# A recurrent stage with the squares of its Newton chain on ScalarE, mixes of 1024 columns, and TensorE's products and transposes of a slot in blocks

## The reference

```python
def step(h, _):
    h = h + 0.01 * jnp.tanh(h)
    h = h * jax.nn.sigmoid(h)
    h = _layernorm(h, ln_w, ln_b)
    h = jnp.einsum('bsc,dc->bsd', h, W) + b
    return (h, None)
x, _ = jax.lax.scan(step, x, None, length=N_ITERS)
...
x = x + _L1_ffn_ref(_layernorm(x, axis=-1), L1_ffn_ln_w, L1_ffn_ln_b, L1_ffn_W, L1_ffn_b)
```

## Time and profile before

| | us |
|---|---|
| median of 3 runs | 3229.25 (3229.11 to 3229.91) |
| the profiled execution, its own time | 3229.77 |
| its span | 3228.0 |
| first three layers, and the start of the recurrent one | 0 to 1806 |
| recurrent layer, step 0 | 1806 to 1894 |
| steps 1 to 29 | 1894 to 3175 |
| last pass | 3175 to 3228 |

### The profile page before, as it was taken

How to read it: one execution, slowest core, us unless ns; L and a number is a source line. 1 busy time by engine, 2 the same in 40 slices (tenths; PEclk the granted TensorE clock), 3 DMA queues, 4 the chain that set the end, 5 groups by cost and what they waited for, 6 DMA issues and landing times. The chain is left out here.

```text
span 3228.0 us, 67245 instructions
## 1 busy us (share of the span) xinstructions
PE 3034.4 (94%) x16801; PEld 2092.0 (65%) x16801; DVE 2831.7 (88%) x8856; ACT 2382.6 (74%) x4988; POOL 1722.1 (53%) x1101
## 2 busy tenths in 40 slices
PE   6999896999999899999999489999999999999997
PEld 4666665888888577777777355555555555555556
DVE  4777776888888788888888779999999999999997
ACT  4666664444444577777777699999999999999993
POOL 2444444333332121211211058899898888888886
PEclk9999997999999999999999589999999999999999
DMA  4000000000000000000000035555555555555557
GB/s 130 17 19 16 16 16 14 1 0 0 0 0 0 25 14 10 13 12 11 13 10 4 3 132 195 198 184 188 198 190 184 197 195 184 190 199 188 187 197 245
DMA packets 135071, 290.03 MB, mean 90 GB/s; under 512 B 12081, under 2 KB 69601, under 8 KB 135009
## 3 DMA queue, kind: packets, MB, share of 16 engines
q1 hardware_dynamic: 118112, 280.89, 25.7%
q10 hardware_dynamic: 16896, 8.39, 0.9%
HBM read 278.88 MB, written 10.35 MB: 90 GB/s over the span
## 5 line engine op out<-in xcount | busy, mean ns | idle before, releaser
L1077 POOL TENSOR_TENSOR d_g<-d_g,d_rb 128x1024 f32<-128x1024 f32 x480 | 1121.1, 2371 | 269.6 <-DMA d_rb<-d_rstd_rows 269.6
L1265 PE MATMUL d_p_y<-d_g,d_w_main 128*128 128x512 f32 x1856 | 960.9, 599 | 0.0
L1279 PEld LDWEIGHTS d_p_gt<-ident,d_g 128*128 128x128 f32 x3840 | 466.0, 142 | 527.7 <-ACT d_g L1324 365.1
L1142 DVE BATCH_NORM_STATS2 d_stats<-d_p_gt 128x6 f32<-128x256 f32 x1920 | 712.7, 407 | 24.1 <-PE d_p_gt L1279 24.1
L1324 ACT ACTIVATE d_g<-d_th,d_bias 128x512 f32<-128x512 f32 x928 | 670.2, 722 | 67.1 <-DVE d_th L1135 37.3
L1135 DVE SCALAR_TENSOR_TENSOR d_th<-d_th,d_p_y 128x512 f32<-128x512 f32 x960 | 638.0, 665 | 4.4 <-ACT d_th L1320 4.3
L1320 ACT ACTIVATE d_th<-d_p_y,d_bias 128x512 f32<-128x512 f32 x928 | 621.7, 670 | 1.3 <-PE d_p_y L1265 1.2
L1279 PE MATMUL d_p_gt<-ident,d_g 128*128 128x128 f32 x3840 | 592.0, 277 | 0.0
L514 ACT ACTIVATE a_prob<-a_masked,a_neg_max 128x128 f32<-128x128 f32 x1024 | 327.4, 391 | 111.5 <-DVE a_neg_max L334 111.4
L434 PE MATMUL a_p_s<-a_k_heads,a_q_t 128*128 128x512 f32 x768 | 397.4, 599 | 0.5 <-DVE a_k_heads L310 0.5
L451 PEld LDWEIGHTS a_p_pv<-a_v_ones,a_prob_t 128*128 128x128 f32 x3072 | 373.7, 192 | 10.7 <-issue 10.3
(11 more groups left out here) (170 smaller groups left out, 4399.5 us busy)
## 6 DMA issues: line engine op xcount, KB each, us to landing
d_rb<-d_rstd_rows SPq DMA_DIRECT2D x480, 512.0 KB, 5.5
a_adj_in<-in_adj_dram SPq DMA_DIRECT2D x64, 256.0 KB, 2.8
out_dram<-d_out_sb ACTq DMA_DIRECT2D x32, 256.0 KB, 3.3
d_rstd_rows<-d_rstd_row SPq DMA_DIRECT2D x120, 16.0 KB, 1.4
m_w_sb<-in_L_ffn_w_dram SPq DMA_DIRECT2D x2, 512.0 KB
x_sb<-in_x_dram SPq DMA_DIRECT2D x1, 256.0 KB, 2.9
a_w_raw<-in_L_gnn_Wq_dram SPq DMA_DIRECT2D x2, 64.0 KB, 2.1
a_w_raw<-in_L_gnn_Wk_dram SPq DMA_DIRECT2D x2, 64.0 KB, 2.1
```

The lines of the kernel that those rows point to most:

```text
L1077: nc.gpsimd.tensor_tensor(g[:, c, :], g[:, c, :], rb[:, buf, :], ALU.mult).then_inc(s_gs, 1)
L1142: ins = nc.vector.bn_stats(stats[:, q % 2, (j * CT + t) // 2].rearrange("p a s -> p (a s)"), p_gt[:, t * P:(t + 2) * P].rearrange("p (a c) ...
L1265: nc.tensor.matmul(p_y[:, c % 2, cols(u)], w_main[:], g[:, c, cols(u)], start=True, stop=True).then_inc(s_y, 1)
L1279: ins = nc.tensor.transpose(p_gt[:, t * P:(t + 1) * P], g[:, c, t * P:(t + 1) * P], ident[:])
```

## The change

VectorE's chain for the reciprocal square root has nine steps instead of ten, by other constants, and steps 2, 4 and 6 of them are squares on ScalarE (`newton_square`), one after the silus of a slot. VectorE mixes a slot in one instruction of 1024 columns, after both tanhs. ScalarE runs tanh u0, tanh u1 of slot s, then silu u0, silu u1 of slot s-1. TensorE runs both products of a slot, then the transposes u0 of slot s-2, in one slot of four the transpose of the reciprocal square roots, then the transposes u1. GpSimd begins scaling when all of x is normalised. The last step's reciprocal square roots are not spread: `last_product` takes the unscaled state, and `add_x` multiplies while it adds, in four instructions of 128x128 per unit instead of one of 128x512; `out_sb` has eight buffers.

```diff
-    CHAIN, XCHAIN, PLACES = 10, 12, 3
+    SPREADS = ALL_GROUPS - GROUPS
+    CHAIN, XCHAIN, PREP = 9, 12, 11
+    PLACES = {(0, 2): 0, (1, 0): 1, (1, 2): 3, (2, 2): 5, (3, 2): 7, (4, 0): 8}
+    ACT_PLACES = {(1, 0): 2, (2, 0): 4, (3, 0): 6}
-    OUTS = 4
+    OUTS = 8
...
-            with eng.Fori(2, ITERS) as i:
+            with eng.Fori(2, ITERS - 1) as i:
                 body(i)
+            body(ITERS - 1)
             body(ITERS)
...
             @block.gpsimd
+                pool.wait_ge(s_xn, CHUNKS * UNITS)
+                pool.wait_ge(s_prep, PREP)
                 with pool.Fori(1, CHUNKS + 1) as i:
                     for c in range(CHUNKS):
                         scale(i, c)
-                    pool.wait_ge(s_prep, 10)
-                    pool.wait_ge(s_xn, CHUNKS * UNITS)
...
-                def mix(s, b, u):
-                    dve.wait_ge(s_th, units(s, u))
+                def mix(s, b):
+                    dve.wait_ge(s_th, units(s, UNITS - 1))
+                    nc.vector.scalar_tensor_tensor(out=th[:, b], in0=th[:, b], scalar=0.01, in1=p_y[:, b],
+                                                   op0=ALU.mult, op1=ALU.add).then_inc(s_u, 1)
...
                 def add_x(o, u):
+                    for t in range(UT):
+                        tile = u * UT + t
+                        ins = nc.vector.scalar_tensor_tensor(
+                            out=out_sb[:, n % OUTS, t * P:(t + 1) * P], in0=p_y[:, o % 2, tile * P:(tile + 1) * P],
+                            scalar=rstd[:, q, o % GC * CT + tile:o % GC * CT + tile + 1], in1=x_sb[:, o * CT + tile, :],
+                            op0=ALU.mult, op1=ALU.add)
...
-                        if live(s - 1):
-                            mix(s - 1, (c - 1) % 2, 1)
-                        elif last(i):
-                            add_x(c - 1, 1)
-                        newton_part(i, c, 0)
                         if live(s - 2):
                             statistics(s - 2, (c - 2) % CHUNKS, 0)
-                        newton_part(i, c, 1)
+                        newton_part(i, c, 0)
                         if live(s):
-                            mix(s, c % 2, 0)
+                            mix(s, c % 2)
                         else:
                             add_x(c, 0)
+                            add_x(c, 1)
+                        newton_part(i, c, 1)
                         if live(s - 2):
                             statistics(s - 2, (c - 2) % CHUNKS, 1)
                         newton_part(i, c, 2)
...
                 def last_product(s, c, u):
-                    pe.wait_ge(s_gs, s - CHUNKS + 1)
+                    pe.wait_ge(s_g, units(s - CHUNKS, u))
...
-                            if live(s - 2):
-                                transpose_g(s - 2, (c - 2) % CHUNKS, u)
-                        k = GROUPS * i + (c - 9) // GC
-                        if c % GC == 1 and live_group(k):
-                            transpose_rstd(k)
+                        if live(s - 2):
+                            transpose_g(s - 2, (c - 2) % CHUNKS, 0)
+                        k, q = GROUPS * i + (c - 10) // GC, (c - 10) // GC % GROUPS
+                        if c % GC == 2 and spread_group(k):
+                            transpose_rstd(k, q)
+                        if live(s - 2):
+                            transpose_g(s - 2, (c - 2) % CHUNKS, 1)
...
+                def newton_square(k, q, n):
+                    act.wait_ge(s_nw, CHAIN * k + n)
+                    if n == 4:
+                        ins = nc.scalar.activation(off, vy2, ACT.Square, bias=centre[:])
+                    else:
+                        ins = nc.scalar.activation(y2[:], rstd[:, q, :], ACT.Square, scale=1.0 if n == 2 else CUBIC)
...
-                        if live(s):
-                            tanh(s, c % 2, 0, col)
-                        if live(s - 1):
-                            silu(s - 1, (c - 1) % CHUNKS, 1, 0.0 if isinstance(i, int) and s - 1 < CHUNKS else bias[:])
+                        for u in range(UNITS):
+                            if live(s):
+                                tanh(s, c % 2, u, col)
+                        for u in range(UNITS):
+                            if live(s - 1):
+                                silu(s - 1, (c - 1) % CHUNKS, u, 0.0 if isinstance(i, int) and s - 1 < CHUNKS else bias[:])
+                        newton_part(i, c, 0)
...
-                        if live(s):
-                            tanh(s, c % 2, 1, col)
-                            silu(s, c, 0, col)
```

More of the change, by code:

```diff
@@ L974, in recurrent_ffn @@
         stats = sb("stats", [P, 2, GTILES // 2, 2, 3])
[L975 to L976 removed]
+        rstd = sb("rstd", [P, GROUPS, GTILES])
+        y2 = sb("y2", [P, GTILES])
+        centre = sb("centre", [P, 1])
         rstd_row = sb("rstd_row", [GTILES, 2, P])
@@ L988, in recurrent_ffn @@
         p_rt = p_row[0:GTILES, 0:P]
-        v, work, v_x, work_x = (p_nw[:, n * GTILES:(n + 1) * GTILES] for n in range(4))
+        v, vy2, off, v_x, work_x = (p_nw[:, n * GTILES:(n + 1) * GTILES] for n in range(5))
         s_load = sem("weights_loaded")
@@ L1027, in live_group, with spread_group @@
             return not isinstance(k, int) or 0 <= k < ALL_GROUPS
+        def spread_group(k):
+            return not isinstance(k, int) or 0 <= k < SPREADS
         def iterations(eng, body):
@@ L1087, in _ @@
                                             ALU.add).then_inc(s_xb, 1)
-                with pool.Fori(CHUNKS + 1, ITERS + 1) as i:
+                with pool.Fori(CHUNKS + 1, ITERS) as i:
                     for c in range(CHUNKS):
@@ L1211, in body @@
                             if c in (0, 1, 4, 5, 8, 9):
-                                for n in range(c % GC * 6, c % GC * 6 + 6):
+                                for n in range(c % GC * 6, min(c % GC * 6 + 6, XCHAIN)):
                                     newton_of_x(1 + c // GC, n)
@@ L1220, in _ @@
                     stats_of_x(GC + c)
-                    for n in range(3 * c, 3 * c + 3):
+                    for n in range(3 * c, min(3 * c + 3, XCHAIN)):
                         newton_of_x(0, n)
@@ L1236, in _ @@
                 link(nc.vector.tensor_copy(bias_bc[:], p_gt[:, P:2 * P]))
+                link(nc.vector.memset(centre[:], -5.0 / 3.0))
                 iterations(dve, body)
-                dve.wait_ge(s_xb, CHUNKS)
-                add_x(CHUNKS - 1, 1)
             @block.tensor
@@ L1254, in bank_taken @@
                     else:
-                        wait(pe, s_u, units(s - 2, u))
+                        wait(pe, s_u, s - 1)
                 def transpose_x(c, u):
@@ L1322, in silu, with newton_part @@
                 def silu(s, c, u, col):
-                    act.wait_ge(s_u, units(s, u))
+                    act.wait_ge(s_u, s + 1)
                     nc.scalar.activation(g[:, c, cols(u)], th[:, c % 2, cols(u)], ACT.Silu, bias=col).then_inc(s_g, 1)
+                def newton_square(k, q, n):
[4 more added lines that the diff above has]
+                        ins = nc.scalar.activation(y2[:], rstd[:, q, :], ACT.Square, scale=1.0 if n == 2 else CUBIC)
+                    ins.then_inc(s_nw, 1)
+                def newton_part(i, c, place):
+                    k, q = GROUPS * i + (c - 5) // GC, (c - 5) // GC % GROUPS
+                    n = ACT_PLACES.get(((c - 5) % GC, place))
+                    if n is not None and live_group(k):
+                        newton_square(k, q, n)
                 def store(o, u):
```

61 lines of the change are left out of this document (26 added, 35 removed).

## The result

The changed kernel takes **3242.98 us** (median of 6 runs, 3241.78 to 3245.20) against 3229.18 (6 runs, 3226.34 to 3231.66): ratio 1.0044, 95% interval 1.0032 to 1.0057. It is slower by 14 us, where the prediction had 3222.0 and a range up to 3238. The profiled execution took 3243.27, its span is 3241.4.

A forecast was written before the change was run, and what follows sets the result against it. VectorE, never waiting in steps 1 to 29, bounds the kernel at 11.07 us per group; after the change a loop gives 11.02. Sum -5.8 + 6 + 1 - 8.5 = -7.3 from 3229.25: 3222.0 us, range 3207 to 3238.

The forecast's parts named there:

- The loop: Steps 1 to 29: TensorE and VectorE wait on each other through one-slot p_gt; 5.42 us per two slots, 10.84 per group.
- 0.05 until the weight load begins: Handover from the end of VectorE's statistics u1 to TensorE's weight load, 0.05 us, read from 12.43 to 12.48.
- The small transpose: TensorE's transpose of the reciprocal square roots, between the two blocks; sticks out a little, within a shared +0.03 per group.
- the chain's first step: VectorE's first reciprocal-square-root step waits for statistics just issued; sticks out, within a shared +0.03 per group (0 to 0.2).
- the branch: Turn of TensorE's instruction loop, once in 16 slots: 0.2 sticks out, +0.05 us per group, between 0 and 0.08.
- ScalarE's load: Steps 1 to 29: three squares add 0.67 to 10.22, giving 10.89 us per group, between 10.64 and 11.38.
- rival 2: The loop does not bind, a wait being released earlier; ScalarE's 10.89 per group decides, 3207 us; chance 0.08.
- The ends: Step 0 +6 us from ScalarE's order and +1 from GpSimd's later scaling; last pass 44.5 instead of 53, -8.5.
- Rival 1: Mix, branch and small transpose cost 0.02 to 0.11 per group more: 3224 to 3235 us, no visible change; chance 0.34.
- rival 3: ScalarE becomes the bound: at 0.385 per square a group costs 11.38, giving 3264 us; chance 0.07.
- Rival 4: TensorE's queue pays more, register work behind waits delaying the product: group 11.2, 3243 us; chance 0.09.
- The rule of the Trainium skill: VectorE's wide mix takes 1.19 us; if the next instruction waited for all, +0.16 per group, near 3240.

The follow-up runs named there:

- stats_first: Changed kernel with VectorE's statistics u1 of slot s-2 ahead of the wide mix of slot s instead of behind it: 3159.01 us, ratio 0.9782 to the kernel before.
- wait_order: Changed kernel with the two waits of transpose_g swapped, first for the statistics, then for the silu: 3243.40 us, ratio 1.0043 to the kernel before.
- interleaved: Changed kernel with TensorE running product u0, transposes u0 of s-2, product u1, then transposes u1: 3298.55 us, ratio 1.0215 to the kernel before.

## Why the prediction was wrong

**The loop** was read rightly: its place, its members and that it binds before any load. What failed is its length. Per turn, predicted and measured in the rows above:

| | predicted | measured |
|---|---|---|
| statistics u1 until done | 0.74 | 0.755 |
| until the weight load | 0.05 | 0.115 |
| load to product | 0.49 | 0.495 |
| products, transposes, start | 2.36 | 2.355 |
| statistics u0, wide mix | 1.78 | 1.80 |
| two slots | 5.42 | 5.52 |

The step that failed is "0.05 until the weight load begins": two thirds of the error of 0.10 come from there, and with them the sign of the result. The term was read from one handover, and that one has another form than the loop's. The trace of the kernel before has two forms (2000 to 3000). 678 weight loads of transposes have the wait for the statistics on an instruction of the queue ahead of them, as have the 336 loads of the changed kernel that begin a second block, all but the one behind each turn of the instruction loop; none of the 678 starts less than 0.115 after the statistics' end, and the median is 0.116. The other 45, two per turn of the instruction loop and the row among them, carry this wait themselves and start after 0.052 to 0.054. The profile puts down to `d_stats` only these 45, since it reads the releaser from the load's own wait, and the 678 to a silu (waits of the kernel before, 2000 to 3000):

```profile
PEld d_p_gt L1279 <- ACT d_g L1324: 286.1, 678, 0.7
...
PEld d_p_gt L1279 <- DVE d_stats L1142: 20.7, 45, 0.5
```

That the form of the wait makes the difference is read from these two groups; no run changed it in the loop. Nor is it shown that the faster form would shorten the loop: in the row a product was still running, and the first transpose began only at 2512.73, 0.30 after the statistics. The rest of the error is the pair's duration (0.015) and the mix's distance of 1.13 instead of 1.11. That term, too, came from one row: the median distance after a mix of 512 columns in the kernel before is 0.595 and not 0.58, and with it the prediction's own rule gives 1.125.

Twice 0.10 makes 0.20 per group. The small transpose and the chain's first step stick out nothing (taken 0.03 together), the branch 0.06 (0.05 taken, right). So 11.02 becomes 11.20, and 0.18 x 116 = 21 us is the whole miss: 3222 + 21 = 3243.

**ScalarE's load** was wrong too, though it decided nothing: the prediction had 10.89 per group as the floor that the loads leave, and `stats_first` runs at 10.48. The squares cost 0.49 and not 0.67, and the other activations less than 0.63 each. So the 3207 of rival 2 was not the least that was to be had.

**The ends** were right. From the first tanh of step 0 to that of step 1 are 95.0 instead of 88.2 (+6.8, predicted +7); from the last slot's tanh to the end 44.1 instead of 52.9 (predicted 44.5), with `add_x` busy for 33.6 us of a stretch of 36.4, 0.26 from start to start as taken, and no wait for stores.

**The rivals.** None names the handover that failed. Rival 1 has the loop right, but its terms (mix, branch, small transpose) came to only 0.02 per group more than taken, of the 0.18. Rival 2 falls with the two runs of one more instruction, rival 3 with the run without squares. Rival 4 looks at the right queue and names the time (3243), but by luck: it prices register work behind the waits, and 0.3 for the small transpose and 0.3 for the branch are not in the trace, where the loss stands ahead of the weight load. The rule of the Trainium skill ("VectorE: DVE Perf Modes", section on the TRN2 errata) gave a time near 3240, closer than the forecast, by luck as well. The mix's duration is 1.21, near the 1.19 of that page, but the next instruction starts after 1.13, so only 0.02 of its 0.08 is there. By the budget of the Trainium skill ("ScalarE: Activation LUTs", rules for kernel authors) for an activation with a pointer bias, a square is estimated at 0.33; the one with a pointer costs 0.25, those without 0.12.

**The range.** It gave the mix 12 us each way and the two readings of the earlier trace rows nothing. A term that is passed twice per group 116 times is worth 2.3 us for each 0.01; 0.05 against 0.115 alone moves the top from 3238 to 3253. And the gain forecast for the loop, 0.05 per group, was smaller than what its terms could be read to.

## What to carry to other kernels

When a change lengthens the queue between "buffer read" and "buffer free", add up the loop through that buffer before the loads; and if it comes out near the load, put the instruction that frees the buffer ahead of the long one (here 84 us for a swap of two lines). Price every handover of such a loop from the median over all its occurrences in the trace, never from one row, nor from those alone that carry the wanted releaser's name; look too whether the waiting instruction carries the wait itself or an instruction of its queue ahead of it does (here 0.053 against 0.115). The term is paid in each turn. A pairing on one engine (tanh, tanh, silu, silu) asks for the matching blocks on the next, and fits one stage and not another: step 0 wanted the silus between the tanhs.

## What the runs showed of the hardware

- A VectorE step of 32 columns with all its operands in SBUF took 1.66 us on average instead of 0.17 where GpSimd scaled rows of 1024 columns beside it, and 0.67 with GpSimd's instructions cut to 0.73. Scratch in PSUM was worth 500 us of 3745.
- From the end of VectorE's statistics to a weight load 0.115 us pass if an `EVENT_SEMAPHORE` of TensorE's queue waits for them ahead of the load (0.114 to 0.117 in 336 cases of the changed kernel), 0.124 if a register instruction of the queue does (`wait_order`, median), and 0.053 if the weight load carries the wait itself (45 cases of the kernel before, 21 of `interleaved`).
- A square of 128x32 takes ScalarE 0.12 without a pointer operand and 0.25 with one. The next instruction after a mix of 1024 columns starts 1.12 to 1.13 after it, while its duration is 1.21.
